# Attention token factors spread over partitions by DMA through device memory instead of diagonals and matmuls

## What is computed

```python
def poincare_fully_connected(x, z, r, c):
    lam = 2.0 / (1.0 - c * sum(x * x, axis=-1, keepdims=True))       # one number for each token
    z_norm = maximum(norm(z, axis=0), EPS)
    inner = x @ (z / z_norm)
    v = 2.0 * z_norm * arcsinh(lam * inner * cosh(2 * r) - (lam - 1.0) * sinh(2 * r))
    w = sinh(v)
    return w / (1.0 + sqrt(1.0 + sum(w * w, axis=-1, keepdims=True)))  # one factor for each token
Q, K = poincare_fully_connected(x, z_q, b_q, 1), poincare_fully_connected(x, z_k, b_k, 1)
V = x @ w_v.T + b_v
out = softmax(Q K^T / 4) V     # 16 heads of 16; x is layer-normalised, out is added to x
```

## Time and profile before

| | us |
|---|---|
| median of 3 runs (lowest, highest) | 2967.22 (2965.24, 2967.39) |
| profiled execution, whole | 2969.68 |
| its span, first to last instruction | 2967.9 |
| busy: PE / ScalarE / DVE / POOL | 2711.7 / 2050.9 / 1865.0 / 1230.1 |
| mean granted TensorE clock | 0.976 of full speed |

### The profile page before, as it was taken

How to read it: one execution, slowest core, us unless ns; L and a number is a source line. 1 busy time by engine, 2 the same in 40 slices (tenths; PEclk the granted TensorE clock), 3 DMA queues, 4 the chain that set the end, 5 groups by cost and what they waited for, 6 DMA issues and landing times. The chain is left out here.

```text
span 2967.9 us, 53759 instructions
## 1 busy us (share of the span) xinstructions
PE 2711.7 (91%) x20801; PEld 1232.0 (42%) x20801; DVE 1865.0 (63%) x2418; ACT 2050.9 (69%) x2696; POOL 1230.1 (41%) x748
## 2 busy tenths in 40 slices
PE   2899999999999999957999999999999998899998
PEld 1456555555555444322333333333333332244443
DVE  8999999999994544465454555555555441235544
ACT  6554554555434565557989898989898998855554
POOL 3889999999993112011504141314232220022200
PEclk7999999999999999978999999999999999999998
DMA  2010010001013121126465544545545456122102
GB/s 85 1 36 26 25 42 28 28 28 35 14 30 114 43 71 42 57 84 114 58 115 87 113 88 102 95 98 93 103 87 100 87 89 151 28 85 73 62 21 71
DMA packets 164050, 201.19 MB, mean 68 GB/s; under 512 B 16504, under 2 KB 118272, under 8 KB 163840
## 3 DMA queue, kind: packets, MB, share of 16 engines
q1 hardware_dynamic: 163840, 198.25, 29.5%
HBM read 139.49 MB, written 58.72 MB: 67 GB/s over the span
## 5 line engine op out<-in xcount | busy, mean ns | idle before, releaser
L2040 ACT ACTIVATE b_pr<-b_ps 128x1024 f32<-128x1024 f32 x1024 | 1000.1, 1035 | 104.2 <-PE b_ps L2108 98.4
L2108 PE MATMUL b_ps<-b_st 128*32 128x512 bf16 x8192 | 613.2, 382 | 47.9 <-ACT b_pr L2040 26.1
L2174 PE MATMUL b_acc<-b_pr,b_vaug 128*32 128x512 f32 x4096 | 530.6, 593 | 3.8 <-DVE b_osb L1865 3.2
L2108 PEld LDWEIGHTS b_ps<-b_st 128*32 128x32 bf16 x8192 | 181.8, 95 | 602.9 <-ACT b_pr L2040 355.7
L1340 PE MATMUL f_po<-f_s,o_weights 128*128 128x512 f32 x768 | 351.9, 600 | 10.2 <-DVE f_xr L1130 6.3
L1118 DVE TENSOR_TENSOR f_turned<-f_cs,f_s 128x1024 f32<-128x1024 f32 x96 | 119.4, 1244 | 367.3 <-ACT f_cs L1243 362.3
L753 PE MATMUL a_pv<-a_xnT,o_big 128*128 128x512 f32 x512 | 248.8, 610 | 55.2 <-DVE a_mem L499 46.0
L1203 ACT ACTIVATE f_h<-f_po,o_weights 128x512 f32<-128x512 f32 x192 | 132.0, 687 | 214.0 <-PE f_po L1340 214.0
L745 PE MATMUL a_pu<-a_xnT,o_big 128*128 128x512 f32 x512 | 234.5, 601 | 31.6 <-DVE o_weights L451 25.7
L1677 POOL TENSOR_TENSOR b_SQ<-o_big 128x1024 f32<-128x1024 f32 x28 | 58.4, 2084 | 465.7 <-DVE o_big L1790 465.7
L1340 PEld LDWEIGHTS f_po<-f_s,o_weights 128*128 128x128 f32 x768 | 140.3, 190 | 213.5 <-issue 158.4
(11 more groups left out here) (288 smaller groups left out, 4529.5 us busy)
## 6 DMA issues: line engine op xcount, KB each, us to landing
b_st<-b_scratch SPq DMA_DIRECT2D x512, 128.0 KB, 7.0
b_scratch<-b_parts SPq DMA_DIRECT2D x32, 768.0 KB, 5.3
o_big<-x SPq DMA_DIRECT2D x16, 1024.0 KB, 6.6
f_xr<-x SPq DMA_DIRECT2D x16, 1024.0 KB, 7.4
a_xl<-in_L_attn_a_x_dram SPq DMA_DIRECT2D x16, 512.0 KB, 4.4
x<-a_xr SPq DMA_DIRECT2D x32, 256.0 KB, 2.2
x<-f_xr SPq DMA_DIRECT2D x8, 1024.0 KB, 4.5
b_xr<-x SPq DMA_DIRECT2D x8, 1024.0 KB, 7.2
```

Source lines behind the costliest of these rows:

```text
L2040: nc.scalar.activation(pr[:, 4 * (blk % 2) + j, :], ps[:, j % 2, :], ACT.Exp, scale=SC).then_inc(S["probs_done"], 1)
L2108: x = nc.tensor.matmul(o[r:r + 32], w[:, r:r + 32], v, start=start, stop=stop, skip_group_check=True)
L2174: x = nc.tensor.matmul(acc[32 * j:32 * j + 32, h * 512:(h + 1) * 512], vaug[:, kt, c:c + 32], pr[:, 4 * (kt % 2) + j, h * 512:(h + 1) * 51 ...
```

## The change

The prologue (batches 0 and 1) keeps its way. In the steady batches `lamb` and `facb` go from the table. SP stores `lam` and each factor column to a row in device memory, element by element, and loads the row back to all partitions; `fac` is the buffer of the former diagonals. `fac` is done for the query (block 17) and the key (block 21) separately; a new step `scale` multiplies one whole feature tile; `split` 0 moves to block 21 and `split` 2 to 24. SP stores and gathers the query's half of the parts before it waits for the key's.

```diff
-    15: [...], 16: [("ln", 3, 1, 0), ("sum", 0, 1, 0), ("sign", 2, 1, 0)], 17: [("up", 3, 1, 0)],
+    15: [...], 16: [("ln", 3, 1, 0), ("sum", 0, 1, 0), ("sign", 2, 1, 0)], 17: [("up", 3, 1, 0), ("fac", 0, 1, 0)],
-    20: [("pair", 1, 1, 0), ("sum", 1, 1, 2)], 21: [("fac", 0, 1, 0)],
-    22: [("facb", 0, 1, 0), ("facb", 1, 1, 2)], 23: [("facb", 2, 1, 0), ("split", 0, 1, 0)], 24: [("facb", 3, 1, 0)],
-    25: [("inT", 0, 2, 0), ("split", 2, 1, 0)], 26: [("inT", 1, 2, 0), ("out", 4, 0, 2)],
+    20: [("pair", 1, 1, 0), ("scale", 0, 1, 0), ("sum", 1, 1, 2)], 21: [("fac", 1, 1, 0), ("split", 0, 1, 0)],
+    24: [("scale", 2, 1, 0), ("split", 2, 1, 0)],
+    25: [("inT", 0, 2, 0), ("scale", 1, 1, 0)], 26: [("inT", 1, 2, 0), ("scale", 3, 1, 0), ("out", 4, 0, 2)],
-    29: [("lamb", 0, 2, 0), ("vaug", 1, 1, 0)], 30: [("lamb", 1, 2, 0), ("split", 3, 1, 0)],
+    29: [("vaug", 1, 1, 0)], 30: [("split", 3, 1, 0)],
...
+    lam_row = nc.dram_tensor("b_lam_row", [T], F32, kind="Internal").ap()
+    fac_rows = nc.dram_tensor("b_fac_rows", [2, T], F32, kind="Internal").ap()
... SP, in batch(b)
                     for g in (2, 3):
+                        if left > 1 and g == 3:
+                            sp.wait_ge(S["lam_done"], 5 * b + 15)
+                            sp.dma_start(lam_row.rearrange("(t p) -> p t", p=P), lam, ...).then_inc(row_stored, 16)
+                            sp.wait_ge(row_stored, 48 * b + 16)
+                            sp.wait_ge(S["a_done"], 8 * b + 16)
+                            sp.dma_start(lamb[:], lam_row.rearrange("(o n) -> o n", o=1).broadcast_to([P, T])).then_inc(row_loaded, 16)
                         sp.wait_ge(S["scores_ready"], 4 * BLK * b + 32 * (g - 1))
                         gather(sp, b, g)
                     if left > 0:
+                        for o in range(2):
+                            sp.wait_ge(S["fac_done"], 4 * b + 2 * o + 6)
+                            sp.wait_ge(S["parts_done"], 4 * b + 4)
+                            sp.dma_start(fac_rows[o].rearrange("(t p) -> p t", p=P), fs[:, 2, o, :], ...).then_inc(row_stored, 16)
+                            sp.wait_ge(row_stored, 48 * b + 16 * o + 32)
+                            sp.wait_ge(row_loaded, 48 * b + 16 * o + 16)
+                            sp.dma_start(fac[o], fac_rows[o].rearrange("(o n) -> o n", o=1).broadcast_to([P, T])).then_inc(row_loaded, 16)
...
-                        store_parts(sp, b + 1, 0)
-                        sp.wait_ge(parts_stored[0], 32 * (b + 2))
+                        store_parts(sp, b + 1, 0, (0,))
+                        sp.wait_ge(parts_stored[0], 32 * b + 48)
                         sp.wait_ge(S["scores_ready"], 4 * BLK * b + 32 * 3)
-                        gather(sp, b + 1, 0)
+                        gather(sp, b + 1, 0, (0,))
+                        store_parts(sp, b + 1, 0, (1,))
+                        sp.wait_ge(parts_stored[0], 32 * b + 64)
+                        gather(sp, b + 1, 0, (1,))
                         store_parts(sp, b + 1, 1)
... POOL
-                        pool.wait_ge(S["fsum_done"], 2 * b + 2)
-                        nc.gpsimd.tensor_tensor(fs[:, 1], fs[:, 0], ..., ALU.pow).then_inc(S["froot_done"], 1)
-                        for o in range(2):
-                            nc.gpsimd.tensor_tensor(dg[:, o], eye, fs[:, 2, o, :]..., ALU.mult).then_inc(S["dfac_done"], 1)
+                        pool.wait_ge(S["fsum_done"], 2 * b + i + 1)
+                        nc.gpsimd.tensor_tensor(fs[:, 1, i], fs[:, 0, i], cst[:, 1:2].broadcast_to([P, NT]), ALU.pow)\
+                            .then_inc(S["froot_done"], 1)
... DVE
-                    if kind == "facb":
-                        o, h = i // 2, i % 2
-                        tile(m)
-                        v = SQ[:, 2 * o:2 * o + 2, h * 512:(h + 1) * 512]
-                        nc.vector.tensor_tensor(v, v, pm[:, par % 2, :].unsqueeze(1).broadcast_to([P, 2, 512]),
-                                                ALU.mult).then_inc(S["misc_taken"], 1)
+                    if kind == "scale":
+                        dve.wait_ge(row_loaded, 48 * b - 16 + 16 * (i // 2))
+                        nc.vector.tensor_tensor(SQ[:, i, :], SQ[:, i, :], fac[i // 2], ALU.mult).then_inc(S["scaled"], 1)
... PE
-                    if kind == "facb":
-                        o, h = i // 2, i % 2
-                        pe.wait_ge(S["dfac_done"], 2 * b + o + 1)
-                        bank_free(m)
-                        x = blocks(bank, ones[:], dg[:, o, 4 * h:4 * h + 4, :].rearrange("p t n -> p (t n)"))
```

More of the change, by code:

```diff
@@ L1443 @@
     14: [("up", 2, 1, 0), ("v", 6, 1, 0), ("pair", 0, 1, 0), ("out", 1, 0, 2)],
-    15: [("down", 2, 1, 0), ("v", 7, 1, 0)], 16: [("ln", 3, 1, 0), ("sum", 0, 1, 0), ("sign", 2, 1, 0)], 17: [("up", 3, 1, 0)],
+    15: [("down", 2, 1, 0), ("v", 7, 1, 0)], 16: [("ln", 3, 1, 0), ("sum", 0, 1, 0), ("sign", 2, 1, 0)], 17: [("up", 3, 1, 0), ("fac", 0, 1, 0)],
     18: [("down", 3, 1, 0), ("out", 2, 0, 2)], 19: [("sign", 3, 1, 0), ("out", 3, 0, 2)],
-    20: [("pair", 1, 1, 0), ("sum", 1, 1, 2)], 21: [("fac", 0, 1, 0)],
-    22: [("facb", 0, 1, 0), ("facb", 1, 1, 2)], 23: [("facb", 2, 1, 0), ("split", 0, 1, 0)], 24: [("facb", 3, 1, 0)],
-    25: [("inT", 0, 2, 0), ("split", 2, 1, 0)], 26: [("inT", 1, 2, 0), ("out", 4, 0, 2)],
+    20: [("pair", 1, 1, 0), ("scale", 0, 1, 0), ("sum", 1, 1, 2)], 21: [("fac", 1, 1, 0), ("split", 0, 1, 0)],
+    24: [("scale", 2, 1, 0), ("split", 2, 1, 0)],
+    25: [("inT", 0, 2, 0), ("scale", 1, 1, 0)], 26: [("inT", 1, 2, 0), ("scale", 3, 1, 0), ("out", 4, 0, 2)],
     27: [("inT", 2, 2, 0), ("vaug", 0, 1, 0), ("out", 5, 0, 2)], 28: [("inT", 3, 2, 0), ("split", 1, 1, 0)],
-    29: [("lamb", 0, 2, 0), ("vaug", 1, 1, 0)], 30: [("lamb", 1, 2, 0), ("split", 3, 1, 0)],
+    29: [("vaug", 1, 1, 0)], 30: [("split", 3, 1, 0)],
     31: [("proja", 0, 2, 0), ("projb", 0, 2, 2), ("vaug", 2, 1, 0)]}
@@ L1459 @@
 STATS_AT, NORM_AT = (15, 16), (21, 22)
-TILE_KINDS = ("inT", "lamb", "projb", "v", "sum", "facb", "out")
+TILE_KINDS = ("inT", "projb", "v", "sum", "out")
 PE_KINDS = TILE_KINDS + ("proja",)
@@ L1529, in phase_b @@
         st_loaded = [s.sem(f"st_loaded{i}") for i in range(2)]
+        row_stored, row_loaded = s.sem("row_stored"), s.sem("row_loaded")
         N_W = 16 * 6
@@ L1616, in batch @@
                     if left > 0:
+                        if left == 1:
+                            sp.sem_inc(row_stored, 16)
+                            sp.sem_inc(row_loaded, 16)
+                        for o in range(2):
+                            sp.wait_ge(S["fac_done"], 4 * b + 2 * o + 6)
+                            sp.wait_ge(S["parts_done"], 4 * b + 4)
+                            sp.sem_inc(passed, 1)
+                            sp.dma_start(fac_rows[o].rearrange("(t p) -> p t", p=P), fs[:, 2, o, :], allow_slow_non_contiguous=True).then_inc(row_stored, 16)
+                            sp.wait_ge(row_stored, 48 * b + 16 * o + 32)
+                            sp.wait_ge(row_loaded, 48 * b + 16 * o + 16)
+                            sp.sem_inc(passed, 1)
+                            sp.dma_start(fac[o], fac_rows[o].rearrange("(o n) -> o n", o=1).broadcast_to([P, T])).then_inc(row_loaded, 16)
                         for q in range(2):
@@ L1720, in _ @@
                 nc.gpsimd.tensor_tensor(znc, znc, cst[:, 1:2].broadcast_to([P, 4]), ALU.pow).then_inc(S["setup_p"], 1)
-                step("lam", 0, 0)
+                step("spread", 0, 0)
                 scales(1)
@@ L1724, in _ @@
                 nc.gpsimd.tensor_tensor(nmr, nmean, rstd, ALU.mult).then_inc(S["nmr_done"], 1)
-                step("lam", 0, 1)
+                step("spread", 0, 1)
                 batch(0, first=True)
@@ L1758, in step @@
                         dve.wait_ge(S["mv_done"], NT * b + NT)
-                        if again(b):
+                        if not isinstance(b, int) or b > 2:
+                            dve.wait_ge(row_stored, 48 * b - 128)
+                        elif b:
                             dve.wait_ge(S["dlam_done"], b)
@@ L1773, in step @@
                         nc.vector.tensor_copy(xnT[:, f, h * 512:(h + 1) * 512], pm[:, par % 2, :]).then_inc(S["misc_taken"], 1)
-                    if kind == "lamb":
-                        tile(m)
[L1776 to L1779, removed]
                     if kind == "projb":
@@ L1783, in step @@
                             dve.wait_ge(S["pair_done"], 2 * b)
+                        if not isinstance(b, int) or b > 1:
+                            dve.wait_ge(row_loaded, 48 * b - 80)
                         q, h = i // 2, i % 2
@@ L1829, in step @@
                     if kind == "fac":
[L1831 to L1836, removed]
-                    if kind == "facb":
-                        o, h = i // 2, i % 2
-                        tile(m)
-                        v = SQ[:, 2 * o:2 * o + 2, h * 512:(h + 1) * 512]
```

(18 more changed lines are left out.)

19 lines of the change are left out of this document (7 added, 12 removed).

## The result

The changed kernel takes 3064.39 us (median of 4, 3061.69 to 3067.09) against 2966.67 of the kernel before in the same comparison: a ratio of 1.0326, 95% interval 1.0312 to 1.034. The forecast was 2955.6 with a range up to 3002. Sign and size were wrong; the time lies beside the upper figure of rival 1, 3069.

What follows compares the result with a forecast made beforehand. ScalarE's exponentials set a block's floor at 3.95 us, and PE's side work beyond its slack lengthens blocks. Removed PE work -22.6 plus copy stall +11.0 gave -11.6: 2967.2 to 2955.6 us, 8-in-10 range 2943 to 3002.

Steps and rivals of the forecast that it cites:

- rival 1: Factors land late for DVE's scale 2, element-wise store slow: 113 us more, 3069, or 46 more, 3002; chance 0.36 for slower.
- I take 4.0, near the lower end: Choice of 4.0 us for the element-wise 4 KB store's landing, between bounds of 2.4 and 12.4.
- Added: two trips through device memory in a chain: Both factors' stores and broadcasts, blocks 20 to 24: nothing late up to S + B of 8.7; 2 us a batch per us above.
- S: Time the 4 KB element-wise store takes to land on an empty ring: 2.4 to 12.4 us, taken as 4.0.
- Removed on PE: `facb` steps of 7 batches and `lamb` steps of 6 go, shortening blocks 22 to 24, 29 and 30: -22.6 us.
- Moved in front of an accumulator copy: DVE's scale 2 and split 2 in block 24 delay block 25's copy; PE stands 1.57 us in 7 batches: +11.0 us.
- B: Time the 512 KB broadcast load of a row to all partitions takes: 3.5 to 7.2 us, taken as 4.4.
- Three diagonals on POOL go too ... at nothing: Removing POOL's three diagonals counted as no gain or loss, since the shortened blocks do not wait for POOL.
- Moved on SP: `lamb` row ahead of group 3's gather: nothing; query half before key half: batch-start wait becomes none, slack over 10 us.
- rival 2: No stall at the accumulator copy, so all 22.6 us stay: 2944.6; chance 0.12.
- rival 3: Factors slightly late, about even: S + B between 9.1 and 9.9, 2961 to 2973 us; chance 0.14.
- rival 4: PE's blocks don't shrink because ScalarE bounds them; only the new stall is left, +11 us; chance 0.02.

## Why the prediction was wrong, step by step

- **The step that failed: "I take 4.0, near the lower end"**, in "Added: two trips through device memory in a chain". S is 9.7 us (median; 8.5 to 10.7), inside the bounds of 2.4 to 12.4, by its formula 2(9.7 + 4.4 - 8.7) = 10.8 us a batch over the limit. With the 1.57 of the copy that makes (10.8 + 1.57) x 7 = 87; measured are 71 in blocks 24 to 26, and 3.2 more that they would have gained. That these are near each other is partly luck. Of waiting for the copy there are only 51.3 us: the second loss lengthens the blocks ahead and gives DVE time (in batch 4 block 20 is 7.1 longer, and scale 2 comes 4.4 late where the formula has 10.8). Another 16.7 go with the fall of the clock around the wait, a term that the sum did not have. The reason for the choice was that the targets are distinct addresses. They are, but only 4 bytes apart, and the spread store shows that the distance counts. The row of 4-byte runs with 2.4 us was a load; a load's price was taken for a store's. The wider mistake was to choose by likeness between ends 10 us apart where the sum turns at 0.8 over.
- **What no step had: PE held while the store is in flight,** 42.7 us in blocks 16 and 20, of which the stops on record make some 25, and where the clock falls behind one the block loses some 2 more. The prediction asked whom the store's landing keeps waiting, not what a slow DMA does to an engine that has nothing to do with it. The time near rival 1's 3069 is thus partly chance: its 113 would have come from the chain alone.
- **"Removed on PE", -22.6:** right. Blocks 22 to 24, 29 and 30 gain 22.7 wherever no store disturbs them.
- **"Moved in front of an accumulator copy", +11.0:** right in place, size and count, 12.0 in the kernel with 32-byte runs. The forecast of -11.6 is about what that kernel would have brought, had block 14 not cost 3.4 and the last batch 3.6, most of this in its wait for a gather (8.7 us for 6.0), which scatters as said; it brought -0.21%, some 6 us.
- **B:** taken as 4.4; 4.2 to 4.5 in batch 4 of after, 3.6 where the ring is not busy. That factor 0's store would stand in the rings behind the gather held too.
- **"Three diagonals on POOL go too ... at nothing":** wrong by 4.4 us. What the `dgl` diagonal's wait for `lam` did was to hold the pair sum back until DVE was through with its addition. In the transposed kernel, where POOL waits for `lam` again, the addition does not take 3.22 any more and block 14 has its old length.
- **"Moved on SP", "turns a wait ... into none":** right in two of seven batches, 3.4 us. The -2.04 of block 31 in batch 0 is something else: there PE stopped for 1.93 us in the profiled execution of before, with no semaphore in the wait (the row at 1522.52), and the four kernels with SP's old order and harmless extra DMAs are 1.1 to 1.9 shorter there too.
- **Rivals 2 to 4:** rival 2 fell with block 25 of the 32-byte kernel, rival 3 with S + B = 14.1, rival 4 with blocks 22 to 30. Rival 1 named the mechanism, the place and what to see (DVE idle before scale 2, released by a DMA).
- **The rules cited.** That a non-contiguous last dimension should be rearranged (the Trainium skill, DMA: Bandwidth & Descriptors, Rules for kernel authors) pointed the right way, and the advice holds here: 0.9928 and 0.9942 come from following it. The reasons that the Trainium skill gives there do not separate the cases: a descriptor for each element cost nothing as a load or spread out, and a price of the read-modify-write under 512 bytes (the Trainium skill, DMA: Bandwidth & Descriptors, Specifications) is not seen in stores of 64-byte pieces (landed in 2.3 us). The S of 2.0 and B of 3.2 that the prediction works out beside its own were both too low for this store and this load: 9.7 and 4.4 were measured.

**What stays open:** why PE stops. In after its stops in block 16 end 7.8 to 9.0 us after the `lam` store's issue, those in block 20 13.9 to 16.4 after the query's, which queues behind the gather, and in the kernel with the extra stores those over 1 us 9.3 to 9.4 after an issue. In the same time packets of the instruction queue are slow. Of its 16 KB packets 12 take over 2 us in after, 15 in the kernel with the changed order and 14 in that with the extra stores, most of them 3.0 to 3.8; in before and in the eight kernels without the dense store none takes over 1.94, with a median of 1.1 to 1.2. That the refill of PE's instruction stream waits behind the store is read from this coincidence and was not isolated. The two do not line up one by one: at five of the nine stops over 1 us in after, the slow packet was still under way when PE went on, and at two there was none; and the profile does not tell whose instructions a packet holds. A late refill would also explain why the `sum` steps are hit, with 64 short multiplications in a row (62 in 0.70 us), which use up instructions fastest; that is argued, not shown.

## What to carry to other kernels

Here a store of a few kilobytes was priced by how its pieces fall into memory, not by its bytes or their number: transpose a 128x8 column on chip first, or let each partition write its 32 bytes as one run (the row then has the tokens in another order, and its reader must want that order). Look for a store that nobody waits for, too: it can still hold an engine, and the clock that falls behind a stop can cost as much again. Where a term's bounds span the point at which the sum turns, forecast the sign with its worse end, and look for the same kind of transfer in the same direction before choosing. When a diagonal, a copy or a tile goes, ask also what its wait was holding apart.

## What the runs showed of the hardware that I had not expected

- Stores of 1024 x 4 bytes, 16 to each 64 bytes of device memory: SP, which waits for the landing, goes on 9.7 us after the issue (8.5 to 10.7, with nothing queued ahead). The packets themselves are through within 2 us of it, so nearly 8 us pass before the landing is seen. Spread out to one for each 64 bytes: 2.9 (median). As a load: 2.4. As 128 runs of 32 bytes: 1.4 to 2.6.
- 18 such stores cost another engine's work 30 us in all, with no dependence between them.
- TensorE's granted clock fell from 2.4 to 1.2 GHz for 3.4 to 10.2 us in or behind idle times of 0.8 to 8.8 us in the middle of attention, 14 times in seven batches, and a multiplication of the weighing took 1.06 us instead of 0.59 in these stretches. It stayed at 2.4 behind stops of 1.81, 1.95 and 2.16 us and waits of 1.48.
- A full 128x1024 addition of DVE took 3.22 us beside a 128x1024 addition of POOL that had begun 0.58 before it (six batches), 1.23 alone.
